# Layer 2 readers placed later in their step, and layer 3 with gate weights spread by DMA and biases on VectorE

## What is computed

```python
x = x + L0(gn(x))      # a Mamba block: projections, a scan over the 2304 pixels, layernorm
x = x + L1(gn(x))      # 1x1 conv, 8x8 FFT filter, 3x3 depthwise conv, gated gelu, 1x1 conv
x = x + L2(gn(x))      # depthwise 11x11 conv, whose kernel comes from 4 points
x = x + L3(gn(x))      # gated mixture of 4 experts
# L3:
scores = softmax(x_flat @ gate_w + gate_b)            # 4 per pixel
top_v, top_i = top_k(scores, 2); top_w = softmax(top_v)
present[k, e] = whether any pixel has expert e at rank k
coef[e, pixel] = sum_k present[k, e] * top_w[k, pixel]
hdn = relu(w1[e] @ x + b1[e])                         # 384 hidden units for each expert
out = sum_e coef[e] * (w2[e] @ hdn + b2[e])
```

## Time and profile before

| | us |
|---|---|
| median of 3 runs | 5612.05 |
| lowest to highest | 5609.07 to 5618.05 |
| profiled execution, its own time | 5612.2 |
| span of its instructions | 5610.3 |

### The profile page before, as it was taken

The page is one execution under the profiler, slowest core; times in us unless marked ns, Lnnn a source line. Parts: engine busy times, 40 slices in busy tenths (PEclk is TensorE's granted clock), DMA queues, the critical chain, the costliest instruction groups (busy, mean ns, idle before and its releaser), DMA issues. The chain is left out here.

```text
span 5610.3 us, 78498 instructions
## 1 busy us (share of the span) xinstructions
PE 4822.8 (86%) x28644; PEld 3822.7 (68%) x28644; DVE 4242.3 (76%) x4727; ACT 3094.3 (55%) x6442; POOL 2967.4 (53%) x3548
## 2 busy tenths in 40 slices
PE   4888888888888888888888877788887979999999
PEld 2666666666666666666666654466665859999998
DVE  1999999999999999999999986666666643333333
ACT  3776777777777777777777743222232323333332
POOL 3776777777777777777777744545443400000000
PEclk8999999999999999999999988798887979999999
DMA  2001000000000010000000012102010101000100
GB/s 74 1 15 29 9 9 10 9 22 22 10 9 10 19 29 14 9 9 10 9 9 10 5 41 80 43 19 75 28 37 15 64 25 33 28 26 28 33 26 22
DMA packets 88527, 136.75 MB, mean 24 GB/s; under 512 B 5285, under 2 KB 85185, under 8 KB 88141
## 3 DMA queue, kind: packets, MB, share of 16 engines
q1 hardware_dynamic: 88140, 131.72, 7.3%
HBM read 89.23 MB, written 42.47 MB: 23 GB/s over the span
## 5 line engine op out<-in xcount | busy, mean ns | idle before, releaser
L743 DVE TENSOR_TENSOR_SCAN a_h<-a_dA,pw 128x771 f32<-128x771 f32 x1152 | 2014.1, 1751 | 121.7 <-PE pw L450 120.8
L599 ACT ACTIVATE a_dA<-a_dt,a_Aneg 128x384 f32<-128x384 f32 x2304 | 1345.2, 607 | 152.4 <-DVE a_h L743 147.4
L461 PEld LDWEIGHTS pw<-g_ident,a_h 128*128 128x128 f32 x6912 | 783.5, 142 | 618.2 <-DVE a_acc L762 268.1
L881 POOL TENSOR_SCALAR a_dBT<-a_dtxT,a_BC 128x768 f32<-128x768 f32 x1152 | 1025.0, 907 | 298.4 <-PE pw L450 213.7
L461 PE MATMUL pw<-g_ident,a_h 128*128 128x128 f32 x6912 | 980.6, 279 | 227.7 <-DVE a_acc L762 157.8
L450 PE MATMUL pw<-g_ident,a_dBT 128*128 128x128 f32 x6912 | 954.2, 275 | 4.8 <-POOL a_dBT L881 4.8
L762 DVE SCALAR_TENSOR_TENSOR a_acc<-pw,a_BC,a_acc 128x768 f32<-128x768 f32 x912 | 913.8, 1002 | 50.9 <-PE pw L461 46.7
L450 PEld LDWEIGHTS pw<-g_ident,a_dBT 128*128 128x128 f32 x6912 | 801.5, 142 | 6.6 <-POOL a_dBT L881 5.5
L1895 DVE TENSOR_TENSOR d_hf<-d_hf,ps 128x384 f32<-128x384 f32 x288 | 159.1, 554 | 566.0 <-ACT d_hf L1825 555.5
L833 POOL TENSOR_TENSOR a_xin<-a_xin,a_tm 128x384 f32<-128x384 f32 x432 | 433.0, 1002 | 34.3 <-ACT a_tm L520 9.0
L893 POOL TENSOR_TENSOR a_acc<-a_acc,a_tm 128x768 f32<-128x768 f32 x168 | 307.0, 1827 | 161.1 <-ACT a_tm L613 160.2
(11 more groups left out here) (243 smaller groups left out, 9365.2 us busy)
## 6 DMA issues: line engine op xcount, KB each, us to landing
b_xs<-x SPq DMA_DIRECT2D x36, 576.0 KB, 4.0
a_xs<-in_x SPq DMA_DIRECT2D x24, 576.0 KB, 4.0
x<-a_xs SPq DMA_DIRECT2D x24, 576.0 KB, 3.0
b_x<-x SPq DMA_DIRECT2D x24, 576.0 KB, 4.6
e_xs<-x SPq DMA_DIRECT2D x24, 576.0 KB, 3.9
out<-e_xs SPq DMA_DIRECT2D x24, 576.0 KB, 3.0
a_sx<-in_x SPq DMA_DIRECT2D x54, 192.0 KB, 2.4
x<-b_x SPq DMA_DIRECT2D x16, 576.0 KB, 3.0
```

The costliest lines, as they stand in the source:

```text
L461: t = e.transpose(m["pw2"][:, c * 128:(c + 1) * 128], m[f"a_h{g % 2}"][:, c // 2, first_col(c) + tb * 128:first_col(c) + (tb + 1) * 128], ...
L599: e.activation(dA[:, first_col(c):first_col(c) + T], m[f"a_dt{k % 2}"][:, c, :], ACT.Exp, scale=m["a_Aneg"][:, c, n:n + 1]).then_inc(s["a_ ...
L743: e.tensor_tensor_scan(m[f"a_h{g % 2}"][:, p % 3, :], m[f"a_dA{pi % NDA}"][:], m[f"pw{pi % 2}"][:, COL:COL + PAIR], 1.0, ALU.mult, ALU.add ...
L881: t = e.tensor_scalar(m[f"a_dBT{g % 2}"][:, tb, :], m[f"a_dtxT{o}"][:, tb, :], m[f"a_BC{o}"][:, tb, n:n + 1], 1.0, ALU.mult, ALU.mult)
```

## The change

Two parts.

**Layer 2.** The unit's readers on ScalarE and VectorE are no longer the main step but generators themselves. For unit u the addition is due at u + 0.8, the patch readers at u + 0.9, the statistics at u + 0.95. So pieces of layer 1 and of the tail due between u and those numbers now come ahead of them. TensorE's and GpSimd's orders in layer 2 stay.

**Layer 3.** The weights are turned once for all chunks by 3 transposes, written to DRAM (`cw`) and read back by one DMA for each chunk, which gives all 128 partitions the chunk's 4 x 384 weights (`d_wb`, three buffers, 768 KB in SBUF for each chunk). VectorE's product reads them from SBUF. The weight matmuls, the small transposes and the bias matmuls leave TensorE. b2 is brought in by three VectorE instructions for each unit (`bias3_dve`), which add weight x b2 to x in place. The gate works on 128 x 288 elements at a time, 26 instructions. `NAHEAD` is 8: eight units of hidden matmuls come ahead of the loop, with 24 `d_hf` buffers; in the loop the order stays as it was, and the units 1 to 7 have no hidden matmuls in it. For this the second chunk is normalized at the start too (`pre3_dve(1)`), ahead of the tail on VectorE.

```diff
-        march(side, UNITS, lambda u: sparse_dve(e, m, w, b, u))
+        march(side + [sparse_dve(e, m, w, b)], 0)
...
-def sparse_act(e, m, w, b, u):
-    for p in unit_patches(u):
-        pixels_act(e, m, w, b, p)
+def sparse_act(e, m, w, b):
+    for u in range(UNITS):
+        for p in unit_patches(u):
+            yield u + 0.9
+            pixels_act(e, m, w, b, p)
...
-NAHEAD = 3
+NAHEAD = 8
+NHF = 3 * NAHEAD
...
     for c in range(CT):
         ps, col = outs3(m)[c], slice(x * C + c * 128, x * C + (c + 1) * 128)
         if x == 0:
             w.wait_ge("v_yo", 3 * (k - 1) + c + 1)
-            w.wait_ge("v_b2r", 3)
-            e.matmul(ps, m["d_b2r"][:, c * 128:(c + 1) * 128], m[f"e_cT{o}"][:], start=True, stop=False, skip_group_check=True)
...
-    by_expert_pe(e, m, w, M, 0)
-    weigh_pe(e, m, w, M, 0)
+    M.claim("a_cT", 1)
+    w.wait_ge("v_sm", GATE_END)
+    for g in range(3):
+        t = e.transpose(m["ps3"][0:96, g * 128:(g + 1) * 128], m["e_co"][:].rearrange("p x n -> p (x n)")[:, 96 * g:96 * (g + 1)], m["g_ident"][:])
+    t.then_inc(m.s["pe_cT"], 1)
     for u in range(NU):
-        k, x = divmod(u, NEXP)
-        if u + 1 < NU:
-            if x == 2 and k + 1 < NCH:
-                by_expert_pe(e, m, w, M, k + 1)
-            weigh_pe(e, m, w, M, u + 1)
-            if u + 1 >= NAHEAD:
-                for i in range(3):
-                    hidden_pe(e, m, w, 3 * (u + 1) + i)
+        if NAHEAD <= u + 1 < NU:
+            for i in range(3):
+                hidden_pe(e, m, w, 3 * (u + 1) + i)
         combine_pe(e, m, w, u)
...
 def scale3_dve(e, m, w, u):
-    w.wait_ge("pe_wg", u + 1)
+    k, x = divmod(u, NEXP)
+    w.wait_ge(f"d_wb{k % 3}", 16 * (k // 3 + 1))
...
-        e.tensor_tensor(f[:], f[:], m["ps3"][:, 0:T], ALU.mult).then_inc(m.s["v_gs"], 1)
+        e.tensor_tensor(f[:], f[:], m[f"d_wb{k % 3}"][:, x, :], ALU.mult).then_inc(m.s["v_gs"], 1)
...
+def bias3_dve(e, m, w, u):
+
+    k, x = divmod(u, NEXP)
+    for c in range(CT):
+        y = m[f"e_xs{k % 3}"][:, c, :]
+        w.wait_ge("v_xn3", 3 * (k + 1))
+        w.wait_ge("v_yb", 3 * (u - 1) + c + 1 if x > 0 else 0)
+        e.scalar_tensor_tensor(out=y, in0=m[f"d_wb{k % 3}"][:, x, :], scalar=m["d_b2"][:, c, x:x + 1], in1=y, op0=ALU.mult, op1=ALU.add).then_inc(m.s["v_yb"], 1)
...
+    def weights(k):
+
+        w.wait_ge("v_yb", 3 * NEXP * (k - 2))
+        w.wait_ge("v_gs", 3 * NEXP * (k - 2))
+        e.dma_start(m[f"d_wb{k % 3}"][:], d["cw"].rearrange("(x n) t -> x (n t)", x=NEXP)[:, k * T:k * T + T].partition_broadcast(128)).then_inc(s[f"d_wb{k % 3}"], 16)
...
+    w.wait_ge("a_cT", 1)
+    e.dma_start(d["cw"].rearrange("(g r) t -> r g t", r=96), m["e_cT"][0:96, :].rearrange("r (g t) -> r g t", g=3)).then_inc(s["d_cw"], 16)
+    w.wait_ge("d_cw", 16)
+    weights(0)
+    weights(1)
     for k in range(NCH):
+        if k + 2 < NCH:
+            weights(k + 2)
```

More of the change, by code:

```diff
@@ L304, in place @@
     m.new("e_xl1", [128, 3, T], F32R)
-    for i in range(9):
+    for i in range(24):
         m.new(f"d_hf{i}", [128, T])
+    for i in range(3):
+        m.new(f"d_wb{i}", [128, 4, T])
     return m
@@ L1454, in head_dve, with sparse_dve @@
         pixels_dve(e, m, w, b, p)
[L1457 to L1474, removed]
+def sparse_dve(e, m, w, b):
+    s = m.s
+    for u in range(UNITS):
+        yield u + 0.8
+        U = UNITS * b + u
+        bi, c = divmod(u, 3)
+        q, j = divmod(bi, 3)
+        y0, y1, v0 = clip(8 * q - 5, 18, H)
+        x0, x1, v1 = clip(16 * j - 6, 28, W)
+        xc = m[f"b_x{b % 2}"][:, c, :]
+        xb = flat(xc)[:, y0:y1, x0:x1]
+        w.wait_ge("pe_s", U + 1)
+        w.wait_ge("p_nb", 12 * (NQ * b + min(NQ, q + 2)))
+        w.wait_ge("v_s", U - 2)
+        e.tensor_tensor(xb, xb, sparse_bank(m, U)[:, v0:v0 + y1 - y0, v1:v1 + x1 - x0], ALU.add).then_inc(s["v_s"], 1)
+        for p in unit_patches(u):
+            yield u + 0.9
+            pixels_dve(e, m, w, b, p)
+        if j == 2:
+            yield u + 0.95
+            w.wait_ge("v_s", U + 1)
+            for i in (q,) if q < NQ - 1 else (q, q + 1):
+                e.bn_stats(m["b_bn3"][:, c, i, :], xc[:, W * BANDS[i][0]:W * BANDS[i][1]]).then_inc(s["v_b3"], 1)
 def tail_dve(e, m, w, b):
@@ L1946, in gate3_dve @@
         if k == 0:
-            for x in range(NEXP):
-                e.scalar_tensor_tensor(out=sc[x], in0=fk[:, k, x, :], scalar=-2.0, in1=sc[x], op0=ALU.mult, op1=ALU.add).then_inc(s["v_sm"], 1)
-    e.tensor_tensor(eq, wk[:, 1, :], wk[:, 0, :], ALU.subtract).then_inc(s["v_sm"], 1)
+            w.wait_ge("v_sm", 10)
+            e.scalar_tensor_tensor(out=coef[:], in0=fk[:, 0, :, :], scalar=-2.0, in1=coef[:], op0=ALU.mult, op1=ALU.add).then_inc(s["v_sm"], 1)
+    w.wait_ge("v_sm", 16)
+    e.tensor_tensor(eq[:], wk[:, 1, :], wk[:, 0, :], ALU.subtract).then_inc(s["v_sm"], 1)
@@ L1985, in l3_dve @@
         if u + 1 < NU:
-            if x == 2 and k + 1 < NCH:
+            if x == 2 and 2 <= k + 1 < NCH:
                 pre3_dve(e, m, w, k + 1)
             scale3_dve(e, m, w, u + 1)
+        bias3_dve(e, m, w, u)
         if x == 3:
```

190 lines of the change are left out of this document (78 added, 112 removed).

## The result

| | before | after |
|---|---|---|
| median, us | 5615.05 (4 runs) | 5387.96 (4 runs, 5384.58 to 5396.13) |
| ratio, 95% interval | | 0.9598 (0.9581 to 0.9614) |
| span of the profiled execution | 5610.3 | 5383.1 |

The change takes 4.0% off. The forecast was 5476 us in a range of 5442 to 5520; the kernel is 54 us faster than the low end. The profiled spans differ by 227.2 us. Three marks divide them: the first unit addition of layer 2, the last one, and the end of the span.

The account below looks back on a forecast made before the run. The prediction took TensorE alone to bound the middle of layer 3, and engines waiting for each other in turn to bound layer 2. From 5612.2 us it summed -117 (loop), -12 (start), +3 (first units), -10 (layer 2) to 5476, range 5442 to 5520.

Parts of the forecast that it names:

- net -10 us, chosen: Layer 2: sooner output additions against later remainders, net 10 us less, from -40 to +35.
- half of the 31 waits, 15 x 1.6 = 25 us: Layer 2: half of TensorE's waits for layer 1's output additions end up to 1.6 us sooner, gaining 25 us.
- The prediction's own sign of being wrong: Layer 2: wrong if the stretch from 3615 us to the layer's end moves by more than 40 us.
- A third of them lose 0.9 us, 16 us: Layer 2: at a third of 54 places, a block's second-unit transposes wait for later remainders, costing 16 us.
- layer 2 gains more: Rival, layer 2: waits and the lower clock go together, 45 us less there, 5440 us; chance 0.10.
- The loop, -117 us: Layer 3's loop: small matmuls and transposes leave TensorE, 4.97 us a chunk, so chunks last 37.5 us; 117 us less.
- Biases at nothing in the loop: Layer 3's loop: twelve VectorE bias instructions a chunk, 5.4 to 9.6 us, stay covered because VectorE is not the bound.
- The start of layer 3, -12 us: Before the loop: first combining matmul 11.3 us later, but 23.5 us of hidden matmuls already done; 12 us less.
- The shorter gate is hidden: Start of layer 3: gate ready at 4582, before hidden tiles end at 4592.2; losing that cover costs 5 us.
- spreading load starved the loop: Rival, layer 3's loop: a chunk lasts as long as its spreading load, 5677 us at 46 us each; chance 0.04.
- wait of VectorE entered the loop: Rival, layer 3: each unit loses 0.6 us in VectorE's chain, 58 us return, 5534 us; chance 0.06.
- readers in layer 2 were not too late: Rival judged, layer 2: late readers make TensorE wait at its transposes, +43 us, 5529 us; chance 0.13.

Follow-up runs that it names:

- add_back: The kernel after, with VectorE's unit addition and statistics due at u again and the patch readers left at u + 0.9: 5449.99 us, ratio 0.9702.
- pix_back: The kernel after, with the patch readers of ScalarE and VectorE due at u again, the addition left at u + 0.8: 5469.89 us, ratio 0.9739.
- add_later: The kernel after, with VectorE's unit addition due at u + 1.3 and statistics at u + 1.35, patch readers at u + 0.9: 5420.78 us, ratio 0.9652.
- small12: The kernel after, with one unused matmul of 12 rows and 384 columns more in each unit of layer 3: 5444.05 us, ratio 0.9687.
- bias_twice: The kernel after, with each VectorE bias instruction in layer 3 run twice, first with a factor of 0: 5404.36 us, ratio 0.9602.
- early_gate: The kernel after, with the gate's pieces on ScalarE and TensorE put among the first 24 hidden tiles: 5373.05 us, ratio 0.9569.
- act_back: The kernel after, with only ScalarE's rounding of the patches due at u again, VectorE's readers staying late: 5373.17 us, ratio 0.9557.

## Why the prediction was wrong

- **Layer 2, "net -10 us, chosen": this is the step that failed**; it measured -96.9. The mechanism for a gain was named (output additions late, convolution done where VectorE stood waiting) but priced wrongly, "half of the 31 waits, 15 x 1.6 = 25 us". The 1.6 us are the readers' own durations. What stood in front of an output was also VectorE's wait for the unit's end, 209 us in 115 places, and the convolution queued behind it. `add_back` and `pix_back` show that this meeting is what costs: bringing back either half returns 57 or 81% of the gain. TensorE's waits for outputs fell by 34.3 us, not 25, those for remainders by 13 and those ahead of the groupnorm sums by 10, together about the 57.3 us of idle time. The bound of -40 was "nearly all of the 48.5", so it came from one group of waits alone, and it held nothing for the clock. The prediction's own sign of being wrong, an end of layer 2 that moves by over 40 us, came true: it moved by 100.
- **"A third of them lose 0.9 us, 16 us": the sign was wrong.** The remainders became due later in the list, but TensorE's waits for them fell by 13 us. VectorE came to them sooner in time.
- **The clock was not in the sum.** The rival "layer 2 gains more" said that waits and the lower clock go together and gave it 45 us and a chance of 0.10, half of what came. About 34 of the 96.9 us are TensorE's same matmuls at a higher granted clock. Every kernel of the table has less idle and less busy time of TensorE than the kernel before, though the two do not rank the kernels alike (`add_later` has less idle time than `add_back` and 2.6 us more busy time). That less idle time is what raises the clock is argued from this; no run held one of them fixed.
- **The loop, -117 us: right.** 37.4 us a chunk against 37.5 forecast, and 0.57 us for a small matmul, confirmed by `small12`. The stretch behind the first combining matmul gained 10 us beyond -114: the +3 us for units 1 to 7 did not come, since TensorE had no idle time in them. The first 44 us of that stretch ran at clock 0.96, where before they ran at 0.82, which is worth about 5 us (an estimate: before, 199 matmuls where the loop's rate gives 236; after, 245 of 255). The rest is 0.1 us a chunk.
- **Biases at nothing in the loop: right**, shown by `bias_twice`, which also shows that the first seven units had little room left. VectorE's 22.6 us a chunk lies in the forecast 22 to 26.
- **The start of layer 3, -12 us: mis-sized**, it measured -2.9. "The shorter gate is hidden" held for VectorE's own work, but the step left out ScalarE: two exponentials are part of the gate, and the first stood behind 24 relus, so the flag sum came 10.93 us behind the hidden tiles. `early_gate` shows that this and the chain behind it cost 20.6 us. From the flag sum to the first product it took 11.6 us where the sum had 12.2, so the DMAs are not what it missed: the spread read took 5.8 us from issue to first product (4508.02 to 4513.80), where the line gave 4.6, and the write 1.9, where it gave 2.4. The fit of the Trainium skill ("DMA: Bandwidth & Descriptors", section "Anatomy of one DMA — SWDGE (gpsimd) path") is given there for DMAs that GpSimd issues, which the prediction did not say; here SyncE issues them. Taken as an estimate all the same it gives 3.8 and 2.3 us, too little for the spread read and too much for the write.
- **A sum that does not come out.** The prediction's "own range" ends at 5525 us; its bounds give 5612.2 - 117 - 5 + 8 + 35 = 5533. The miss is on the other side, so nothing hangs on it.
- **The rivals.** No spreading load starved the loop: the median landing was 5.8 us of the 43 it could have taken, and the first of the three issued together landed in 5.7 us. No wait of VectorE entered the loop, where TensorE was busy 700 of 700 us. The readers in layer 2 were not too late on balance, but `act_back` shows that ScalarE's rounding was: it cost 20.6 us.

## What to carry to other kernels

A reader placed directly behind the work that it reads makes its engine meet the end of that work. Where both engines have other work, put the reader part of a step later (0.4 and 0.8 did nearly the same here), all readers of the busy engine together, and not over a whole step, or the buffer's next writer waits. Try each engine by itself: here it was VectorE whose readers had to move, and ScalarE's did better where they stood. Look for such a move at the engine's idle time at the reader and at what is queued behind it, not at the reader's own duration, and allow for what the clock may give back. This case gives no formula for the price: VectorE's waits at the addition fell by 171.5 us, TensorE's idle time by 57.3. When work is marched ahead of a serial chain, follow the chain through every engine's list: one instruction of it left behind the new work undoes the cover.

## What the runs showed of the hardware

- A matmul of 12 rows and 384 columns between matmuls of 128 rows cost 0.57 us of TensorE's time, one of 128 rows at the same place 0.17.
- By a change of order alone the granted clock in layer 2, which was 0.84 to 0.87 in its first three images, became 0.90 to 0.92. TensorE's busy time for the same 4426 matmuls fell by 39.5 us, of which the clock explains about 34 (estimate above).
- One DMA that gives 128 partitions the same 6 KB (768 KB in SBUF) landed in a median of 5.8 us, a load of 576 KB of separate data in 3.8. The store of 576 KB that is issued 1.4 us behind such a spreading load landed in 5.8 us, and in 3.0 before, without one.
